# Queue order around the macaron kernel's second attention: feed-forward units spread over eight drain rounds, the layer norm moved one round earlier, the low part of x ahead of the low part of y

## The chip, the cores and the metric

One NeuronCore of one Trainium2 chip runs the whole program. The metric is the device time in microseconds (us) of one execution; the time of a kernel is the median of its runs.

## The reference, cut to what matters

The input x has 8192 tokens of 256 channels. Six residual stages follow each other: a gated feed-forward with 4-bit quantization, a decaying linear attention, the same feed-forward again, a ternary feed-forward, a linear attention with a compressive memory, and the ternary feed-forward again. The change touches the fifth stage and the beginning of the sixth.

```python
def _L1_attn_ref(hidden_states, w_q, w_k, w_v, w_o, gate, memories, memory_norms):
    q, k, v = (proj(w_q), proj(w_k), proj(w_v))
    sq = elu1(q)
    sk = elu1(k)
    out_m = jnp.einsum('bhsd,mhde->mbhse', sq, memories)
    rel = jnp.einsum('bhsd,mhd->mbhs', sq, memory_norms)
    out_m = out_m / jnp.clip(rel, EPS, None)[..., None]
    weights = jax.nn.softmax(rel.mean(axis=-1), axis=0)
    mem_out = jnp.einsum('mbhse,mbh->bhse', out_m, weights)
...
    num = jnp.einsum('bhsd,bhsde->bhse', sq, kv_cum)
    den = jnp.clip(jnp.einsum('bhsd,bhsd->bhs', sq, k_cum), EPS, None)
    local = num / den[..., None]
    out = g * mem_out + (1.0 - g) * local
    return out @ w_o.T

def _L1_ffn_ref(x, W1, b1, W2, b2):
    h = jnp.einsum('bsd,fd->bsf', x, _ternary(W1)) + b1
    h = jax.nn.gelu(h, approximate=False)
    return jnp.einsum('bsf,df->bsd', h, _ternary(W2)) + b2
...
    x = x + _L1_attn_ref(_layernorm(x, axis=-1), ...)
    x = x + 0.5 * _L1_ffn_ref(_layernorm(x, axis=-1), ...)
```

## The kernel before, in words

x stays in SBUF as 64 tiles of 128 tokens; four tiles are a chunk. Each engine runs a list of instructions written out by hand, in order, and semaphores tie the lists together. Most products are made from a high and a low part of an operand, so a tile that PE transposes into PSUM is first copied by ACT as the high part (`XTH`, `YTH`), and then DVE subtracts that from PSUM to get the low part (`XTL`, `YTL`).

The second attention is a software pipeline of rounds n = 0 to 75. With j = n % 4, round n does on PE, in this order: `values(n)` and, 12 tiles behind, `out_proj(n - 12)`; `keys(n)`; `grow`, `numerators`; `recall(n - 10)` (the memory part); `denominators`, `scores(n)`, `enter`; transposes of tile n - 2's numerators and of y of tile n - 11 into one pair of banks called "l"; at j = 0 the transposes of the next chunk of x (`turn_x`); at j = 1 and 2 halves of the next chunk's projection (`attn1_proj`); at n % 8 == 1 (n > 8) a sum over eight tiles ("w") for the softmax weights. From n = 64 on there are no new tiles: round 64 has what is left of tile 63, and rounds 65 to 75 are the drain, which has `recall` (to round 73), `out_proj` and the transposes of y, and, between them, the first units of the next feed-forward.

All of it shares three pairs of PSUM banks, handed out in the order of `slots1()`; in rounds 66 and later only two pairs, in turn, since the feed-forward needs two banks. `attn1_take` makes PE wait until the last user of the pair is emptied. Worked out from that order: from round 12 on, the second half of `recall(n - 10)` takes the pair of `values(n)`, which ACT's copy L2009 (`VK1`) empties. `out_proj(z)` also waits for `s_yl`, which DVE's L2139 (`YTL`) gives in the round before. In rounds 67 to 73 the first half of `recall` needs the pair that `residual` (DVE L2069) of the round before empties, and its second half the pair that L2139 of the round before empties; `out_proj` then needs the first half of the same round's `recall` emptied by DVE (L2086, `recalled`).

A feed-forward unit (`ffn1_unit`, one per 128 of 1024 hidden channels of a chunk) is four matmuls of 512 columns (L1559, L1560) on PE, a gelu (L1599) and a copy (L1603) on ACT, and a subtraction (L1625) on DVE; from unit 5 on PE also does the eight matmuls (L1576, L1578) of the unit five before. Units 0 to 10 of stage 5 are placed in the drain rounds by the table `beside`; unit 11 and all later ones follow the last `out_proj`. Units 5, 6 and 7 are followed on ACT by one row each of a layer norm, and so is unit 8; units 0 to 2 on DVE by its statistics.

`norm` (ACT L267, four activations) writes the normalized next chunk, `XN`, that `turn_x` transposes at the next j = 0. `low(i)` (DVE L290, two subtractions) makes the low part of that chunk once ACT has copied the high part (L286). It is needed by `attn1_proj` a round later.

Of the kernel before, what the change touches and what calls it, by code (L numbers as in the profile page):

```python
# [7 lines left out]
NT = 64  # L8
# [17 lines left out]
def macaron(nc, x, wgu, wd, wqkv, bqkv, bv, wo0, bo0, gam, w1, b1, w2, b2, aw, awo, gate, mem, mnorm, cst, out):  # L26
    pwd = nc.dram_tensor("pw_scratch", [16, 256], F32, kind="Internal").ap()
    top = ExitStack()
    with top:
# [225 lines left out]
        def norm(act, S, i, rows=range(4)):  # L255
            F = 16 * S + i
            b = F % 2
            if 0 in rows:
                act.wait_ge(s_nb, 2 * F + 2)
                if S in (0, 2) and i:  # L260
                    act.wait_ge(s_qxv, 8 * S + i)
                elif S in (1, 3) and i == 0:
                    act.wait_ge(s_qxv, 8 * (S - 1) + NS)
                elif F:
                    act.wait_ge(s_xt, 2 * F)
            for j in rows:
                t = act.activation(XN[:, j, :], X[:, 4 * i + j, :], ACT.Identity,  # L267
                                   scale=rs[b][:, j:j + 1], bias=nb[b][:, j:j + 1])
            if 3 in rows:
                t.then_inc(s_xn, 1)  # L270
# [1414 lines left out]
        after1 = lambda j: 15 * (j // 16) + min(j % 16 + 1, 15)  # L1685

        beside = {66: (0, 1), 67: (2, 3), 68: (4, 5), 69: (6, 7), 70: (8,), 71: (9,), 72: (10,)}
        AHEAD = 11

        def slots1():
# [79 lines left out]
        def attn1_pe(pe):  # L1771
# [124 lines left out]
            for n in range(NT + FAR + 2):  # L1896
                m, p, r, y, z, i, j = n - 1, n - 2, n - FAR, n - FAR - 1, n - FAR - 2, n // 4 + 1, n % 4
                if n > NT and r < NT:
                    recall(r)
                for u in beside.get(n, ())[:1]:  # L1900
                    ffn1_unit(pe, 5, u)
                if n < NT:
                    values(n)
                if z >= 0:
                    out_proj(z)
                if n < NT:
                    keys(n)
                if n == 0:
                    turn_x(i)
                if n == 1:  # L1910
                    pe.wait_ge(s_xd, 64 * 3 + 64)
                if 0 <= m < NT:
                    grow(m, 0)
                    numerators(m)
                if n <= NT and r >= 0:
                    recall(r)
                if 0 <= m < NT:
                    denominators(m)
                    grow(m, 1)
                if n < NT:  # L1920
                    scores(n)
                if 0 <= m < NT:
                    enter(m)
                if 0 <= p < NT or 0 <= y < NT:
                    bank = attn1_take(pe, "l", n)
                if 0 <= p < NT:
                    pe.wait_ge(n_nu, p + 1)
                    for c in range(3):
                        t = pe.transpose(bank[:, 128 * c:128 * c + 128], NU[p % 2][:, 128 * c:128 * c + 128],
                                         ident[:, :])  # L1930
                    t.then_inc(n_lx, 1)
                if 0 <= y < NT:
                    pe.wait_ge(n_p, 3 * y + 3)
                    for k in range(2):
                        t = pe.transpose(bank[:, 512 + 128 * k:640 + 128 * k], Y[y % 2][:, 128 * k:128 * k + 128],
                                         ident[:, :])
                    t.then_inc(n_yx, 1)
                for u in beside.get(n, ())[1:]:
                    ffn1_unit(pe, 5, u)
                if 0 < n <= NT and j == 0:  # L1940
                    turn_x(i)
                if n < NT and i < NS and j in (1, 2):
                    attn1_proj(pe, i, j - 1)
                if n % 8 == 1 and 8 < n < NT + 2:
                    bt = n // 8 - 1
                    bank = attn1_take(pe, "w", bt)
                    pe.wait_ge(n_le, p + 1)
                    for c in range(8):
                        raw = L[:, (8 * bt + c) % 10, 256:336].rearrange("p (q c) -> p q c", q=4)
                        t = pe.matmul(bank[:, 0:64], ones[:, :], raw[:, :, 4:20], start=(c == 0), stop=(c == 7))  # L1950
                    t.then_inc(n_rsum, 1)
# [9 lines left out]
        def attn1_act(act):  # L1961
# [40 lines left out]
            for n in range(NT + FAR + 2):  # L2002
                m, p, y, i, j = n - 1, n - 2, n - FAR - 1, n // 4 + 1, n % 4
                if n < NT:
                    act.wait_ge(n_vk, n + 1)
                    if n > 1:
                        act.wait_ge(n_up, after1(2 * (n - 2) + 1))
                        act.wait_ge(d_v1[n % 2], 64 * ((n - 2) // 2) + 64)
                    act.activation(VK1[n % 2][:, 0:512], pair1("v", n)[:, 0:512], ACT.Copy).then_inc(n_vke, 1)  # L2009
                    if j == 2:  # L2010
                        norm(act, *chunk(64 + i + 1))
                if n == 66:
                    act.wait_ge(n_lx, NT)
                for u in beside.get(n, ())[:1]:
                    ffn1_unit_act(act, 5, u)
                if 0 <= m < NT:
                    act.wait_ge(n_it, m + 1)
                    if m > 1:
                        act.wait_ge(n_lx, m - 1)
                    act.activation(NU[m % 2][:, :], PS[6][:, 0:384], ACT.Copy).then_inc(n_nu, 1)  # L2020
                if 0 <= y < NT:
                    act.wait_ge(n_yx, y + 1)
                    if y:
                        act.wait_ge(n_op, y)
                    act.activation(YTH[:, :], half1(1, "l", n)[:, 0:256], ACT.Copy).then_inc(s_yh, 1)
                for u in beside.get(n, ())[1:]:
                    ffn1_unit_act(act, 5, u)
                if 0 <= p < NT:
                    act.wait_ge(n_lx, p + 1)
                    if p > 9:  # L2030
                        act.wait_ge(n_p, 3 * (p - 10) + 3)
                    act.activation(L[:, p % 10, 0:256], half1(0, "l", n)[:, 0:256], ACT.Copy)
                    act.activation(L[:, p % 10, 256:336].rearrange("p (q c) -> p q c", q=4),
                                   half1(0, "l", n)[:, 256:384].rearrange("p (q c) -> p q c", q=4)[:, :, 0:20],
                                   ACT.Copy).then_inc(n_le, 1)
                if n <= NT and j == 0:
                    turn_x(i)
                if n < NT and i < NS:
                    if j in (1, 2):
                        proj(i, j - 1)  # L2040
                    if j == 3:
                        keys(i)
                if n % 8 == 1 and 8 < n < NT + 2:
                    bt = n // 8 - 1
                    act.wait_ge(n_wz, 7 * bt + 3)
                    act.activation(RM[bt % 2][:, :], RM[bt % 2][:, :], ACT.Exp).then_inc(n_wx, 1)
        def attn1_dve(dve):
            v3 = lambda a: a.rearrange("p (g m b) -> p g m b", m=4, b=2)
            vm = lambda a: a.rearrange("p (g m b) -> p g b m", m=4, b=2)
# [21 lines left out]
            def mask(n, g):  # L2071
                dve.wait_ge(n_sc, 2 * n + g + 1)
                if n:
                    dve.wait_ge(n_av, n)
                tab = bass.AP(tensor=TR[:, :].tensor, offset=TR[:, :].offset,
                              ap=[list(TR[:, :].ap[0]), [0, 2], [0, 4], [1, 64]])
                dve.tensor_tensor(
                    a1A[:, 512 * g:512 * g + 512].rearrange("p (q a t) -> p q a t", q=2, a=4),
                    pair1("s", n, g).rearrange("p (q c) -> p q c", q=2)[:, :, 0:256].rearrange(
                        "p q (a t) -> p q a t", a=4), tab, ALU.mult).then_inc(n_am, 1)  # L2080
# [14 lines left out]
            for n in range(NT + FAR + 2):  # L2095
# [31 lines left out]
                    recalled(r, 1)  # L2127
                if 0 < n <= NT:
                    state(2 * n - 1)
                for u in beside.get(n, ())[:1]:  # L2130
                    ffn1_unit_dve(dve, 5, u)
                if n > NT:
                    residual(z)
                if n < NT:
                    mask(n, 0)
                    mask(n, 1)
                if 0 <= y < NT:
                    dve.wait_ge(s_yh, NT + y + 1)
                    dve.tensor_tensor(YTL[:, :], half1(1, "l", n)[:, 0:256], YTH[:, :].bitcast(F32),  # L2139
                                      ALU.subtract).then_inc(s_yl, 1)  # L2140
                if n <= NT and j == 0:
                    low(i)
                for u in beside.get(n, ())[1:]:
                    ffn1_unit_dve(dve, 5, u)
                if 0 <= p < NT:
                    dve.wait_ge(n_le, p + 1)
# [171 lines left out]
```

## Time and profile before

| | us |
|---|---|
| median of 3 runs (lowest, highest) | 2545.09 (2544.83, 2546.74) |
| the profiled execution, its own time | 2546.74 |
| its span in the trace | 2544.7 |
| PE matmuls busy | 2413.9 |
| DVE busy | 1889.8 |
| ACT busy | 1407.7 |

Rounds can be counted by ACT's 64 copies L2009: the one of round n is the (n+1)th. The first starts at 1654.41 us and the last, of round 63, at 2225.49 us. The first instruction of unit 11 starts at 2300.95 us.

### The profile page before, as it was taken

Reading aid. Unit: us, or ns where it says so; the run is one execution under the profiler, and the core shown is the slowest. Engines: PE = TensorE matmul, PEld = TensorE weight load, DVE = VectorE, ACT = ScalarE, POOL = GpSimd, SP = SyncE. Lnnn points to the kernel's source line nnn. Section 1 sums busy time; section 2 is a strip of 40 time slices with the busy share of each in tenths; the row PEclk is TensorE's granted clock in tenths of the full one; section 3 lists DMA queues with packets and bytes.
Section 4 is the critical chain, followed back from the end, with each engine's and each line's share of the span. In section 5 each row is a group of like instructions: output and inputs, shape, how many; then the busy total and the mean of one; then the engine's idle time right before and its main releaser. Section 6 shows DMA issues by size and latency. Waiting matters only on the chain.

```text
span 2544.7 us, 78166 instructions
## 1 busy us (share of the span) xinstructions
PE 2413.9 (95%) x32232; PEld 2119.3 (83%) x32232; DVE 1889.8 (74%) x4447; ACT 1407.7 (55%) x2427; POOL 1287.2 (51%) x1392
## 2 busy tenths in 40 slices
PE   4999999999999979999999999989999999989999
PEld 3888888888888868888888899877888888868998
DVE  8999899677778789999985766546666666665664
ACT  4555555533434435556655888854444445436886
POOL 5878888621212138889996333113443444444331
PEclk9999999999999999999999999999999999989999
DMA  5000000001111110000000000000000000000111
GB/s 190 1 7 1 1 1 1 1 23 24 24 24 25 24 48 1 1 1 1 1 1 1 19 1 2 1 20 18 17 18 18 17 18 17 18 4 26 34 34 42
DMA packets 67728, 46.12 MB, mean 18 GB/s; under 512 B 13216, under 2 KB 66352, under 8 KB 67376
## 3 DMA queue, kind: packets, MB, share of 16 engines
q1 hardware_dynamic: 67376, 41.13, 5.7%
q8 instruction: 257, 4.21, 0.7%
q14 instruction: 95, 0.78, 0.1%
HBM read 15.91 MB, written 8.40 MB: 10 GB/s over the span
## 4 chain that ended last, share of the span: by engine, by line
PE 85%; DVE 5%; issue 3%; POOL 3%; ACT 3%; DMA 0%; SPq 0%; DVEq 0%; ACTq 0%; POOLq 0%
PE ps L46 14%; PE ps L48 13%; PE ps L47 13%; PE ps L1576 5%; PE ps L1578 5%; PE ps L1559 5%; PE ps L1560 4%; PE ps L628 3%; PE ps L280 3%; PE ps L1856 3%; PE ps L1135 2%; PE ps L1167 2%; PE ps L1816 1%; PE ps L1891 1%; PE ps L1874 1%
## 5 line engine op out<-in xcount | busy, mean ns | idle before, releaser
L1625 DVE TENSOR_TENSOR gHl<-gHf,gHh 128x512 fp32r<-128x512 f32 x256 | 186.3, 728 | 192.9 <-ACT gHh L1603 192.8
L46 PE MATMUL ps<-WGH,XTH 128*128 128x512 f32 (+1 forms) x768 | 300.0, 391 | 7.3 <-ACT fSG L697 4.5
L247 POOL TENSOR_SCALAR ve<-mv 128x4 f32<-128x4 f32 x96 | 22.0, 229 | 558.8 <-DVE mv L237 554.5
L48 PE MATMUL ps<-WGL,XTH 128*128 128x512 f32 (+1 forms) x768 | 290.2, 378 | 0.0
L47 PE MATMUL ps<-WGH,XTL 128*128 128x512 f32 (+1 forms) x768 | 289.4, 377 | 0.0
L697 ACT ACTIVATE fSG<-ps 128x704 f32<-128x704 f32 x128 | 97.0, 758 | 311.2 <-PE ps L48 311.2
L843 POOL TENSOR_TENSOR fHTL<-fHTF,fHTH 128x768 fp32r<-128x768 f32 x128 | 235.8, 1842 | 63.4 <-ACT fHTF L706 63.4
L1576 PE MATMUL ps<-W2T,gHh 128*128 128x256 f32 x1024 | 256.9, 284 | 0.0
L1578 PE MATMUL ps<-W2T,gHl 128*128 128x256 f32 x1024 | 254.3, 282 | 0.0
L1599 ACT ACTIVATE gHf<-ps,B 128x512 f32<-128x512 f32 x256 | 175.9, 687 | 92.2 <-PE ps L1560 88.2
L46 PE MATMUL ps<-WDH,fHTH 128*128 128x256 f32 x768 | 221.8, 289 | 2.6 <-issue 2.6
L48 PE MATMUL ps<-WDL,fHTH 128*128 128x256 f32 x768 | 216.4, 282 | 0.0
L47 PE MATMUL ps<-WDH,fHTL 128*128 128x256 f32 x768 | 216.2, 281 | 0.0
L267 ACT ACTIVATE XN<-X,nb,rs 128x256 f32<-128x256 f32 x384 | 209.4, 590 | 7.7 <-POOL nb L253 7.7
L1559 PE MATMUL ps<-XTH,W1T 128*128 128x512 f32 x512 | 208.6, 407 | 0.4 <-DVE XTL L290 0.4
L1560 PE MATMUL ps<-XTL,W1T 128*128 128x512 f32 x512 | 203.8, 398 | 0.0
L1576 PEld LDWEIGHTS ps<-W2T,gHh 128*128 128x128 f32 x1024 | 194.1, 190 | 10.6
L849 POOL TENSOR_TENSOR fV<-fH,frc 128x704 f32<-128x704 f32 x128 | 178.1, 1391 | 48.8 <-DVE frc L788 48.4
L1578 PEld LDWEIGHTS ps<-W2T,gHl 128*128 128x128 f32 x1024 | 193.4, 189 | 9.2
L855 POOL TENSOR_TENSOR fHX<-fV,fsc 128x704 f32<-128x704 f32 x128 | 178.0, 1390 | 28.3 <-DVE fV L322 28.3
L1603 ACT ACTIVATE gHh<-gHf 128x512 fp32r<-128x512 f32 x256 | 161.7, 632 | 8.2
L46 PEld LDWEIGHTS ps<-WGH,XTH 128*128 128x128 f32 x768 | 145.9, 190 | 23.0 <-ACT fSG L697 6.0
(257 smaller groups left out, 7084.6 us busy)
## 6 DMA issues: line engine op xcount, KB each, us to landing
X<-in_x SPq DMA_DIRECT2D x16, 512.0 KB, 8.8
a0vp<-a0vt SPq DMA_DIRECT2D x256, 32.0 KB
a1vp<-a1vk SPq DMA_DIRECT2D x256, 32.0 KB, 1.9
out<-X SPq DMA_DIRECT2D x16, 512.0 KB, 2.9
tws<-in_w SPq DMA_DIRECT2D x2, 1024.0 KB, 7.8
WN<-in_wgu SPq DMA_DIRECT2D x3, 384.0 KB, 5.6
a0km<-in_wqkv SPq DMA_DIRECT2D x2, 384.0 KB, 3.3
a1pry<-in_aw SPq DMA_DIRECT2D x1, 768.0 KB, 4.6
```

Source lines behind the costliest of these rows:

```text
L46: e.matmul(o, hh, mh, start=first, stop=False)
L47: e.matmul(o, hl, mh, start=False, stop=False)
L48: return e.matmul(o, hh, ml, start=False, stop=last)
L267: t = act.activation(XN[:, j, :], X[:, 4 * i + j, :], ACT.Identity, scale=rs[b][:, j:j + 1], bias=nb[b][:, j:j + 1])
L843: pool.tensor_tensor(HTL[(n - 3) % 2][:, :, :], HTF[:, :, :], HTH[(n - 3) % 2][:, :, :].bitcast(F32), ALU.subtract).then_inc(s_hlo, 1)
L849: pool.tensor_tensor(s3(V[n % 2][:, :]), s3(H[n % 2][:, :]), cast16(rc[n % 2][:, :], 44), ALU.mult).then_inc(s_hv, 1)
L855: pool.tensor_tensor(s3(HX[(n - 1) % 2][:, :]), s3(V[(n - 1) % 2][:, :]), cast16(sc[(n - 1) % 3][:, :], 44), ALU.mult).then_inc(s_hx, 1)
L1559: pe.matmul(up(S, m)[:, :], W1T[:, k, fs], XTH[b][:, k, :], start=(k == 0), stop=False)
L1560: t = pe.matmul(up(S, m)[:, :], W1T[:, k, fs], XTL[b][:, k, :], start=False, stop=(k == 1))
L1576: pe.matmul(o, Hh[S][w][:, js], W2T[:, f, :], start=(f == 0 and j % 2 == 0), stop=False, skip_group_check=True)
L1578: t = pe.matmul(o, Hl[S][w][:, js], W2T[:, f, :], start=False, stop=(f == 7), skip_group_check=True)
L1625: dve.tensor_tensor(Hl[S][m % 8][:, :], Hf[S][m % 4][:, :], Hh[S][m % 8][:, :].bitcast(F32), ALU.subtract).then_inc(s_hl, 1)
```

## The change

The units of `beside` are spread over eight rounds in place of seven, one unit in the even and two in the odd rounds up to 71, and all of a round's units come at the end of the round, behind the transposes and copies of y. Before, the first unit of a round stood between `recall` and `out_proj` on PE, ahead of the copies for y on ACT and ahead of `residual` and `YTL` on DVE. The norm on ACT goes from round j = 2, behind the copy L2009, to the very end of round j = 1. On DVE `low(i)` goes ahead of `YTL` in rounds j = 0. Nothing is computed that was not computed before.

```diff
-        beside = {66: (0, 1), 67: (2, 3), 68: (4, 5), 69: (6, 7), 70: (8,), 71: (9,), 72: (10,)}
+        beside = {66: (0,), 67: (1, 2), 68: (3,), 69: (4, 5), 70: (6,), 71: (7, 8), 72: (9,), 73: (10,)}
@@ attn1_pe
                 if n > NT and r < NT:
                     recall(r)
-                for u in beside.get(n, ())[:1]:
-                    ffn1_unit(pe, 5, u)
                 if n < NT:
                     values(n)
@@ behind the transposes of y
-                for u in beside.get(n, ())[1:]:
+                for u in beside.get(n, ()):
                     ffn1_unit(pe, 5, u)
@@ attn1_act
                     act.activation(VK1[n % 2][:, 0:512], pair1("v", n)[:, 0:512], ACT.Copy).then_inc(n_vke, 1)
-                    if j == 2:
-                        norm(act, *chunk(64 + i + 1))
                 if n == 66:
                     act.wait_ge(n_lx, NT)
-                for u in beside.get(n, ())[:1]:
-                    ffn1_unit_act(act, 5, u)
                 if 0 <= m < NT:
                     act.wait_ge(n_it, m + 1)
@@ behind the copy YTH
-                for u in beside.get(n, ())[1:]:
+                for u in beside.get(n, ()):
                     ffn1_unit_act(act, 5, u)
@@ behind the exponential L2046, the last of the round
+                if n < NT and j == 1:
+                    norm(act, *chunk(64 + i + 1))
@@ attn1_dve
                 if 0 < n <= NT:
                     state(2 * n - 1)
-                for u in beside.get(n, ())[:1]:
-                    ffn1_unit_dve(dve, 5, u)
                 if n > NT:
                     residual(z)
                 if n < NT:
                     mask(n, 0)
                     mask(n, 1)
+                if n <= NT and j == 0:
+                    low(i)
                 if 0 <= y < NT:
                     dve.wait_ge(s_yh, NT + y + 1)
                     dve.tensor_tensor(YTL[:, :], half1(1, "l", n)[:, 0:256], YTH[:, :].bitcast(F32),
                                       ALU.subtract).then_inc(s_yl, 1)
-                if n <= NT and j == 0:
-                    low(i)
-                for u in beside.get(n, ())[1:]:
+                for u in beside.get(n, ()):
                     ffn1_unit_dve(dve, 5, u)
```

## Rows read from the trace of the kernel before

**Rows 1.** The page: busy time, share of the span, instructions.
```profile
PE 2413.9 (95%) x32232; PEld 2119.3 (83%) x32232; DVE 1889.8 (74%) x4447; ACT 1407.7 (55%) x2427; POOL 1287.2 (51%) x1392
```
**Rows 2.** Windows: stretch, its length, busy of PE, PEld, DVE, ACT, POOL; clock; DMA.
```profile
1950.00:2050.00 100.00, 96.99 (x2257) 82.85 (x2257) 65.93 (x163) 47.79 (x105) 40.63 (x61) 1.00 0.07 17
```
**Rows 3.** Waits of PE, 1800 to 2100 us: total, times, longest.
```profile
PE ps L1891 <- ACT a1vk L2009: 5.1, 8, 0.7
```
**Rows 4.** Timeline, rounds 28 and 29: start, duration, engine, line, [idle before, releaser].
```profile
1906.65 0.42 DVE L2139 TENSOR_TENSOR a1ytl<-ps,a1yth 128x256 fp32r<-128x256 f32 x1 [0.86 <-ACT a1yth L2025]
...
1907.54 1.29 DVE L290 TENSOR_TENSOR XTL<-ps,XTH 128x512 fp32r<-128x512 f32 x2 [0.47 <-ACT XTH L286]
1907.60 0.28 PE L46 MATMUL ps<-a1oh,a1yth 128*128 128x256 f32 x1
```
**Rows 5.** Timeline, the change from round 29 to 30.
```profile
1918.56 0.63 ACT L1983 ACTIVATE a1sq<-a1sq 128x512 f32<-128x512 f32 x1
...
1919.55 0.60 ACT L2009 ACTIVATE a1vk<-ps 128x512 f32<-128x512 f32 x1 [0.36 <-PE ps L1801]
...
1920.04 2.06 ACT L267 ACTIVATE XN<-X,nb,rs 128x256 f32<-128x256 f32 x4
...
1920.51 0.73 PE L1891 MATMUL ps<-a1mb,a1sq 32*128 32x128 f32 x16
```
**Rows 6.** Timeline, the change from round 33 (n % 8 == 1) to 34.
```profile
1957.60 0.26 ACT L2046 ACTIVATE a1rm<-a1rm 128x64 f32<-128x64 f32 x1 [2.05 <-DVE a1rm L2172]
1957.77 0.58 ACT L2009 ACTIVATE a1vk<-ps 128x512 f32<-128x512 f32 x1
...
1958.66 0.73 PE L1891 MATMUL ps<-a1mb,a1sq 32*128 32x128 f32 x16
```
**Rows 7.** Timeline, the beginning of round 28.
```profile
1900.94 0.59 ACT L2009 ACTIVATE a1vk<-ps 128x512 f32<-128x512 f32 x1
...
1901.68 0.73 PE L1891 MATMUL ps<-a1mb,a1sq 32*128 32x128 f32 x16 [0.63 <-ACT a1vk L2009]
```
**Rows 8.** Timeline of PE, drain rounds 66 to 75.
```profile
2251.43 0.41 PE L46 MATMUL ps<-a1oh,a1yth 128*128 128x256 f32 x1
...
2256.68 1.24 PE L1891 MATMUL ps<-a1mb,a1sq 32*128 32x128 f32 x16 [2.70 <-DVE a1ytl L2139]
...
2280.82 0.73 PE L1891 MATMUL ps<-a1mb,a1sq 32*128 32x128 f32 x16 [2.25 <-DVE a1ytl L2139]
2281.48 0.50 PE L1559 MATMUL ps<-XTH,W1T 128*128 128x512 f32 x1
...
2282.51 0.28 PE L1576 MATMUL ps<-W2T,gHh 128*128 128x256 f32 x1
...
2286.33 0.94 PE L1891 MATMUL ps<-a1mb,a1sq 32*128 32x128 f32 x16 [1.79 <-DVE a1ytl L2139]
...
2299.53 0.55 PE L46 MATMUL ps<-a1oh,a1yth 128*128 128x256 f32 x1 [1.02 <-DVE a1ytl L2139]
```
**Rows 9.** Timeline of ACT in the drain.
```profile
2251.72 1.28 ACT L1599 ACT_TABLE_LOAD   x1 [2.67 <-PE ps L1560]
...
2282.71 0.69 ACT L1599 ACTIVATE gHf<-ps,B 128x512 f32<-128x512 f32 x1 [3.72 <-PE ps L1560]
2283.43 0.64 ACT L1603 ACTIVATE gHh<-gHf 128x512 fp32r<-128x512 f32 x1
```
**Rows 10.** Timeline of DVE in the drain.
```profile
2284.10 0.77 DVE L1625 TENSOR_TENSOR gHl<-gHf,gHh 128x512 fp32r<-128x512 f32 x1 [1.15 <-ACT gHh L1603]
...
2293.45 1.29 DVE L2086 TENSOR_TENSOR a1P<-ps,a1cf 128x512 f32<-128x512 f32 x2 [0.86 <-DVE a1cf L2117]
```
**Rows 11.** Timeline of PE: single gaps of the other stages, one of six.
```profile
945.14 0.63 PE L280 MATMUL ps<-ident,fXV 128*128 128x128 f32 x4 [1.70 <-DVE XTL L290]
```
**Rows 12.** Windows of PE around such a gap and one in the drain: length, busy, clock, DMA.
```profile
943.00:949.00 6.00, 4.22 (x24) 1.00 0.00 0
2284.00:2290.00 6.00, 4.21 (x30) 0.73 0.01 3
```

## The prediction

> **What bounds the kernel now.** The page comes first: PE matmuls are busy 95% of the span, far ahead of DVE and ACT [rows 1], so what counts is what opens or closes a gap on PE. The windows come next: in the steady part of the second attention, rounds of about 9.5 us, PE is busy 96.99 of 100 us at clock 1.00 [rows 2]. PE's waits there are short; the largest group is `recall` (L1891) behind ACT's copy L2009, 8 times, 0.7 us at most [rows 3]. PE has no slack, and those loops of dependence start and end on PE, so a new wait of PE is hardly given back later. The reader is to look at each of the three moves by one question: whom does PE wait for just there, and how long before PE came had it been ready? The timelines answer that.
>
> **Move 1: `low` ahead of `YTL` (j = 0).** In round 28 DVE does L2139 at 1906.65 for 0.42 us, then the pair L290 from 1907.54 to 1908.83, which must wait for ACT's copies of the high part. PE starts `out_proj` of round 29 at 1907.60 [rows 4]. `out_proj` needs L2139. Once L290 stands ahead of it, L2139 starts at 1908.83 at the earliest and ends at 1909.25. PE starts about 0.15 us behind a release: a copy that ended at 1901.53 let `recall` start at 1901.68 [rows 7]. So `out_proj` starts at 1909.40 and not at 1907.60, 1.80 us later. Who profits? `attn1_proj` needs L290, but it comes a whole round later, and L290 waits for ACT and so starts no earlier than before. There is no gain to set against the loss. Behind the waiting L2139 on DVE stand only the reciprocals of `RC`; behind the waiting PE stands everything. The pattern repeats in rounds 12, 16, ..., 60, which is 13 times: 13 x 1.80 = 23.4 us. In round 64 both `recall` and `out_proj` of round 65 need it; there `recall` comes 2 us later, but DVE's `recalled` only about 0.7 us later, since it had waited for other work. Move 1: **+24 us**. Its bounds: 0 if DVE could do L2139 in the 0.47 us it waits for L286, which its fixed order excludes, up to 26 if a late `residual` costs a little more.
>
> **Move 2: the norm at the end of round j = 1.** Before, its 2.06 us lie behind the copy L2009, in a stretch where ACT waits for PE anyway. After, they lie ahead of that copy, and `recall` (its second half takes the copy's PSUM pair) waits for it. In the even kind of round, ACT's exponential ends at 1919.19 [rows 5]. Neighbouring activations overlap by about 0.1 us (the copy starts at 1919.55, takes 0.60, the norm starts at 1920.04 [rows 5]). So the norm runs 1919.09 to 1921.15, the copy 1921.04 to 1921.64, and `recall` starts at 1921.79 and not at 1920.51: 1.28 us, in rounds 14, 22, ..., 54, six times: 7.7 us. Where n % 8 == 1, the exponential of the weights L2046 ends at 1957.86 and the copy starts right behind it [rows 6]. The norm goes between them: copy to 1960.32, `recall` at 1960.47 and not at 1958.66: 1.81 us, in rounds 18, 26, ..., 58, six times: 10.9 us. Round 62 has no projection ahead of it, so ACT is idle early: 0.3 us. In round 10 it is `scores`, later in the round, that takes the pair: 0.6 us. Rounds 2 and 6: nothing. The copy also starts the DMAs of `VP1`, needed a round later; they shift together with PE. A gain, ACT being free in round j = 2, is worth nothing: it waits for PE there. Move 2: **+19.5 us**, bounds 11 (the six largest alone) and 26 (13 times 2.0). That a copy behind other ACT work stalls `recall` is seen already: in rounds j = 0 it does, for 0.63 us [rows 7].
>
> **Move 3: the units in the drain.** Before, DVE's `YTL` stands behind the first unit's L1625, and so the next `recall` waits for gelu, copy and subtraction: 2.70, 2.25 and 1.79 us [rows 8], 6.7 us together. After, these three waits go. What is late next? The round's last L1625 now stands ahead of the next round's L2086 on DVE, and `out_proj` needs L2086. The length of a round, `out_proj` to `out_proj`, is a chain: `out_proj` and the transposes 0.9; the unit's four matmuls 1.03 (2281.48 to 2282.51 [rows 8]); 0.2 to ACT; gelu and copy 1.36 (2282.71 to 2284.07 [rows 9]); L1625 0.7; the coefficients 0.25; the first half of L2086 0.65 [rows 10]; 0.2 for two handovers: 5.3 us. A second unit adds another 0.94 us of matmuls, and more if the first has its down part in between (another 0.94): 6.7 (units 4, 5) and 7.2 (7, 8). The first two intervals, at half clock, with the table load of 1.28 us [rows 9] and the softmax weights ahead, I put at 8.6 and 8.3. Then 5.3, 6.7, 5.3, 7.2, 5.3, and 5.2 for the last two, which have no `recall`: 51.9 us. Before it was 2299.53 - 2251.43 = 48.1 [rows 8]. The last `out_proj` then runs at the full clock, 0.7 us quicker. Move 3: **+3 us**, from -7 (the three waits go and nothing takes their place) to +8 (half clock throughout the drain). The Trainium skill ("ScalarE: Activation LUTs", What ACT_TABLE_LOAD costs) puts a switch of tables at 2.66 us, with a drain; the trace shows the gelu directly behind a load of 1.28 us, so the row stands. By the page the sum would be 1.4 us higher.
>
> **The clock.** Moves 1 and 2 make 25 new gaps of about 1.3 to 1.8 us. In the trace seven single gaps of 1.4 to 1.8 us bear on it. Six, in other stages, left the clock at 1.00 (one is 1.70 us [rows 11], its window [rows 12]); the one of 1.79 us in the drain [rows 8] was followed by half clock, 0.73 over 6 us, which costs 6 x 0.27 = 1.6 us [rows 12]. One in seven of 25 at 1.6 us is **+6 us**; bounds 0 and 25 x 1.6 = 40.
>
> **The sum:** 24 + 19.5 + 3 + 6 = 52.5 us on the profiled execution's 2546.7 us gives 2599; that execution lies 1.7 above the median of 2545.1, which gives 2597.6. I take **2598 us**.
>
> **The rivals.**
> *Half clock in the attention.* The new gaps lie among matmuls on 32 rows or columns, not among full ones as those six did. If each of them, or most, is followed by half clock, the term of 6 becomes 25 to 40: 2617 to 2632 us. Against it: the 0.63 us waits among the same small matmuls leave it at 1.00.
> *Only one move tells.* Should a later wait absorb one of the two (say `recall`'s stall is taken up by scores and masks), 22 us are left: 2567. Against it: `scores` starts right behind PE's own work in these rounds, and the short waits [rows 3] are too small to absorb anything.
> *No effect.* DVE and ACT find both a place without PE waiting, and the drain comes out even: 2545. It would need the order on each engine not to bind.
> *Faster, by the drain.* The mechanism is that `YTL` no longer waits for the gelu: PE's three waits, 6.7 us, go, and L2086 comes in time; the stalls of moves 1 and 2 don't occur. 2538 us. It decides from the point where the chain of a one-unit round is below PE's own work in it, about 3.5 us (recall 0.7, the chain's 0.9 and 1.03, the down part 0.94); I count 5.3, so even the drain alone is not faster, and it would have to outweigh 43 us besides.
>
> **How the numbers follow.** The forecast, all four terms as worked out within their nearer bounds (2580 to 2616 us): 0.70. Half clock: 0.14. One move alone: 0.08. No effect: 0.04. Faster: 0.04. For 8 in 10 the range goes from 2567, the one-move case, to 2636, the half-clock case with the drain's upper bound. Changes below 0.2% (5 us) can't be told from none. Faster 0.04, the same 0.04, slower 0.92.
>
> **What the profile after would show.** Move 1: at the start of each round j = 1, `out_proj` (L46 from a1yth) with an idle time of 1.8 us, released by DVE a1ytl, 13 times. Move 2: L1891 idle for 1.3 and 1.8 us in turn behind ACT a1vk in rounds j = 2, and ACT's norm ahead of that copy. Move 3: `recall`'s waits for a1ytl gone in the drain, and `out_proj` waiting for DVE a1P or a1pry, 1 to 3 us, in nearly every round; unit 11 starting some 46 us later than before, 3 of it from the drain. The windows of the steady part: PE busy near 92 of 100 us. Wrong would be: no wait on a1ytl in rounds j = 1 (then L2139 is not what `out_proj` waits for), the clock below 0.95 in the steady windows, or a drain below 48 us.

## The result and the profile after

The changed kernel takes 2609.91 us (median of 4 runs, 2605.24 to 2614.76) and the kernel before 2545.91 us on the same chip: ratio 1.0249, 95% interval 1.0225 to 1.0273, so 64 us slower. The forecast was 2598 us, slower, with a range from 2567 to 2636. The profiled execution took 2608.26 us, its span 2606.3. Line numbers have moved a little: after, L2007 is the copy L2009, L2136 is `YTL` (L2139 before), and L2083 is `recalled` (L2086 before).

The windows of the steady part come first, one row of each kernel (stretch, length, busy of PE, PEld, DVE, ACT, POOL, then the clock). Of before:

```profile
1755.00:2215.00 460.00, 443.83 (x10674) 379.92 (x10663) 302.64 (x746) 216.83 (x470) 192.89 (x295) 1.00 0.07 17
```

Of after:

```profile
1755.00:2215.00 460.00, 413.60 (x9608) 352.36 (x9604) 273.17 (x669) 195.83 (x425) 174.66 (x268) 0.97 0.06 16
```

In the same 460 us PE is busy for 30 us less, and its mean clock is 0.97 and no longer 1.00. The waits of PE over the second attention and the drain, 1650 to 2370 us, of after (total, times, longest) say behind whom:

```profile
PE ps L46 <- DVE a1ytl L2136: 27.0, 30, 1.5
PE ps L1891 <- ACT a1vk L2007: 26.1, 26, 1.7
PE ps L46 <- DVE a1P L2083: 9.1, 4, 3.1
PE ps L46 <- DVE a1pry L2083: 8.3, 4, 3.0
...
PE ps L1891 <- DVE a1ytl L2136: 2.2, 1, 2.2
```

and of before, 1650 to 2310 us:

```profile
PE ps L1891 <- ACT a1vk L2009: 8.3, 13, 0.7
PE ps L46 <- DVE a1ytl L2139: 7.9, 18, 1.0
PE ps L1891 <- DVE a1ytl L2139: 7.9, 5, 2.7
```

Each of the three moves has its row. `out_proj` behind `YTL` has grown from 7.9 to 27.0 us (move 1), `recall` behind the copy from 8.3 to 26.1 us (move 2), and the waits of `recall` for `YTL`, 7.9 us, are down to one of 2.2 us, in round 65, while 17.4 us of `out_proj` behind `recalled` have come (move 3).

Round 29 after, which answers to [rows 4] (timelines of DVE and PE):

```profile
1928.40 1.29 DVE L290 TENSOR_TENSOR XTL<-ps,XTH 128x512 fp32r<-128x512 f32 x2 [1.76 <-ACT XTH L286]
1929.61 0.41 DVE L2136 TENSOR_TENSOR a1ytl<-ps,a1yth 128x256 fp32r<-128x256 f32 x1
...
1930.17 0.35 PE L46 MATMUL ps<-a1oh,a1yth 128*128 128x256 f32 x1 [1.54 <-DVE a1ytl L2136]
```

L2136 now starts where L290 ends, and PE 0.15 us behind its end. The idle column says 1.54 us, but the distance of this round's copy from the same one before grows by 1.77 us. Before, the matmul ahead of `out_proj` started at 1907.49 and lasted 0.28 us, while `out_proj` started at 1907.60: 0.17 us of the two were counted together, and that overlap goes too. The round from 29 to 30, which answers to [rows 5]:

```profile
1940.63 0.63 ACT L1981 ACTIVATE a1sq<-a1sq 128x512 f32<-128x512 f32 x1
1941.17 2.06 ACT L267 ACTIVATE XN<-X,nb,rs 128x256 f32<-128x256 f32 x4
1943.14 0.57 ACT L2007 ACTIVATE a1vk<-ps 128x512 f32<-128x512 f32 x1
...
1943.86 0.73 PE L1891 MATMUL ps<-a1mb,a1sq 32*128 32x128 f32 x16 [1.20 <-ACT a1vk L2007]
```

and from 33 to 34, which answers to [rows 6]:

```profile
1983.31 2.06 ACT L267 ACTIVATE XN<-X,nb,rs 128x256 f32<-128x256 f32 x4
1985.28 0.57 ACT L2007 ACTIVATE a1vk<-ps 128x512 f32<-128x512 f32 x1
...
1986.00 0.73 PE L1891 MATMUL ps<-a1mb,a1sq 32*128 32x128 f32 x16 [1.73 <-ACT a1vk L2007]
```

The norm stands between the exponential and the copy, and `recall` is idle for 1.20 or 1.73 us. In the drain, PE of after ([rows 8] before):

```profile
2316.54 0.58 PE L46 MATMUL ps<-a1oh,a1yth 128*128 128x256 f32 x1 [3.06 <-DVE a1P L2083]
...
2324.59 0.39 PE L46 MATMUL ps<-a1oh,a1yth 128*128 128x256 f32 x1 [2.96 <-DVE a1pry L2083]
...
2363.12 0.36 PE L46 MATMUL ps<-a1oh,a1yth 128*128 128x256 f32 x1 [1.02 <-DVE a1ytl L2136]
```

Where the time is, all kernels side by side. The stretches run between starts: of the copy of rounds 0, 12 and 63, of the first `out_proj` of rounds 66 and 75, and of unit 11. All values are of the one profiled execution of each kernel, in us.

| kernel | round 0 at | rounds 0 to 12 | 12 to 63 | 63 to 66 | drain 66 to 75 | to unit 11 | unit 11 to end |
|---|---|---|---|---|---|---|---|
| before | 1654.4 | 96.0 | 475.1 | 25.9 | 48.1 | 1.4 | 243.8 |
| after | 1654.6 | 100.8 | 529.4 | 24.3 | 54.1 | 0.8 | 242.4 |
| e1_low | 1650.6 | 97.4 | 500.5 | 23.9 | 47.7 | 0.8 | 242.4 |
| e2_norm | 1656.7 | 100.2 | 507.7 | 24.9 | 48.0 | 0.8 | 242.4 |
| e4_low_norm | 1655.4 | 99.0 | 528.7 | 26.1 | 46.8 | 1.4 | 243.5 |
| e3_drain | 1649.7 | 96.7 | 473.7 | 25.4 | 56.9 | 1.0 | 243.7 |
| e5_norm_behind | 1655.9 | 96.5 | 472.8 | 25.6 | 46.5 | 1.4 | 243.3 |
| e6_order | 1654.8 | 98.5 | 473.0 | 24.9 | 54.2 | 1.4 | 244.4 |
| e7_table | 1652.0 | 95.4 | 472.6 | 26.1 | 45.5 | 1.4 | 243.1 |
| e8_dve | 1651.1 | 96.6 | 472.0 | 24.6 | 43.3 | 1.4 | 243.4 |
| f1_low_clamp | 1655.3 | 95.7 | 501.7 | 23.8 | 46.0 | 1.4 | 243.1 |
| f2_keys | 1649.5 | 95.1 | 463.6 | 25.1 | 46.5 | 1.4 | 243.1 |
| f3_keys_dve | 1653.7 | 94.8 | 463.7 | 26.1 | 42.5 | 1.4 | 243.2 |
| f4_keys_dve_table | 1655.1 | 97.8 | 466.1 | 25.5 | 45.0 | 1.4 | 243.3 |

Two traces of the same code differ, too. In the six kernels that add no wait to the steady part (before, e3_drain, e5 to e8) rounds 12 to 63 took 472.0 to 475.1 us, and in the seven with the drain of before it took 46.0 to 48.1 us. The trace of before has the largest value both times, so a stall or a loss worked out against it can be up to 3 us too small in the steady part, and a gain in the drain up to 2 us too large.

From before to after: 0.2 + 4.8 + 54.3 - 1.6 + 6.0 - 0.6 - 1.4 = 61.7 us, the difference of the spans. Nearly nine tenths of it is the steady part, where moves 1 and 2 act.

### The profile page after: what moved, and what is told of

The parts are those of the page before. It is cut to its first block, busy times and chain, and to the rows that moved or that the text cites. A ratio compares the mean times of both kernels' runs of the same rounds, so it can differ in the third digit from the quotient of the medians.

```text
span 2606.3 us, 78165 instructions
## 1 busy us (share of the span) xinstructions
PE 2432.0 (93%) x32232; PEld 2133.7 (82%) x32232; DVE 1891.5 (73%) x4447; ACT 1406.7 (54%) x2427; POOL 1285.8 (49%) x1392
## 4 chain that ended last, share of the span: by engine, by line
PE 83%; DVE 6%; ACT 5%; issue 4%; POOL 2%; DMA 0%; SPq 0%; DVEq 0%; ACTq 0%; POOLq 0%
PE ps L46 13%; PE ps L48 13%; PE ps L47 13%; PE ps L1576 5%; PE ps L1578 5%; PE ps L1559 5%; PE ps L1560 4%; PE ps L628 3%; PE ps L280 3%; PE ps L1856 3%; PE ps L1135 2%; PE ps L1167 2%; PE ps L1891 2%; PE ps L1874 1%; PE ps L1154 1%
## 5 line engine op out<-in xcount | busy, mean ns | idle before, releaser
L1625 DVE TENSOR_TENSOR gHl<-gHf,gHh 128x512 fp32r<-128x512 f32 x256 | 184.9, 723 | 195.8 <-ACT gHh L1603 195.7
L843 POOL TENSOR_TENSOR fHTL<-fHTF,fHTH 128x768 fp32r<-128x768 f32 x128 | 235.8, 1842 | 61.7 <-ACT fHTF L706 61.7
L2014 ACT ACTIVATE a1nu<-ps 128x384 f32<-128x384 f32 x64 | 31.4, 491 | 271.0 <-PE ps L1880 271.0
```

Source lines behind the costliest of these rows:

```text
L843: pool.tensor_tensor(HTL[(n - 3) % 2][:, :, :], HTF[:, :, :], HTH[(n - 3) % 2][:, :, :].bitcast(F32), ALU.subtract).then_inc(s_hlo, 1)
L1625: dve.tensor_tensor(Hl[S][m % 8][:, :], Hf[S][m % 4][:, :], Hh[S][m % 8][:, :].bitcast(F32), ALU.subtract).then_inc(s_hl, 1)
```

## The experiments

Times are medians; the ratio is to the kernel before, run beside it on the same chip, with its 95% interval. The median of before was 2543.2 us beside e1 to e8 and 2542.1 us beside f1 to f4.

**e1_low, move 1 alone.**

```diff
+                if n <= NT and j == 0:
+                    low(i)
                 if 0 <= y < NT:
                     dve.wait_ge(s_yh, NT + y + 1)
...
-                if n <= NT and j == 0:
-                    low(i)
```

> Only move 1 of the change (DVE's low, L290, ahead of YTL). Theory (order on DVE delays out_proj): out_proj of each round j = 1 stands idle about 1.5 us behind YTL, 13 times, each round 1.8 us late, 24 us in all, plus 0 to 6 us where the clock falls: 2568 to 2576 us. Rival (the stall is absorbed later in the round): within 3 us of the kernel before.

Measured 2572.94 us, 1.0118 (1.0090 to 1.0146). Rounds 12 to 63 take 25.4 us more than before. Its waits of PE, 1750 to 2250 us:

```profile
PE ps L46 <- DVE a1ytl L2141: 24.5, 27, 1.5
PE ps L1891 <- ACT a1vk L2009: 7.7, 12, 0.7
```

The first row holds the 13 long waits, the second is that of before. 13 x 1.77 = 23.0 us is the stall, 2.4 us is left for the clock. The trace is of the fastest execution, 2565.29 us at a mean clock of 0.989; the other three took 2570 to 2579 us at 0.985 or 0.986, so in them the clock probably cost more. The stall is not absorbed; the rival falls.

**e2_norm, move 2 alone.**

```diff
-                    if j == 2:
-                        norm(act, *chunk(64 + i + 1))
...
                     act.activation(RM[bt % 2][:, :], RM[bt % 2][:, :], ACT.Exp).then_inc(n_wx, 1)
+                if n < NT and j == 1:
+                    norm(act, *chunk(64 + i + 1))
```

> Only move 2 (the norm at the very end of ACT's round j = 1, so ahead of the copy VK1 of round j = 2). Theory: recall of rounds j = 2 idle behind that copy, 1.2 us in six rounds and 1.7 us in six, 19.5 us in all, plus 0 to 6 us of clock: 2564 to 2572 us. Rival (ACT has slack enough, its share of busy time being 55%): within 3 us of the kernel before.

Measured 2582.38 us, 1.016 (1.014 to 1.018), more than either theory gave. Its waits of PE, 1750 to 2265 us:

```profile
PE ps L1891 <- ACT a1vk L2009: 25.9, 25, 1.7
PE ps L46 <- DVE a1ytl L2140: 4.9, 15, 0.3
```

The waits are as expected. Rounds 12 to 63 take 32.6 us more. The twelve stalls at the forecast's size, 6 x 1.28 + 6 x 1.81, and 0.3 in round 62 are 18.8 of them; about 14 us are left. The windows of PE around round 18 show where they are:

```profile
1808.00:1818.00 10.00, 9.94 (x182) 1.00 0.05 13
1818.00:1828.00 10.00, 8.33 (x154) 0.66 0.06 16
1828.00:1838.00 10.00, 9.67 (x226) 1.00 0.06 16
```

and its timeline what half clock does to small matmuls, 1.99 us for the 32 of `scores` in place of 1.12 us:

```profile
1819.67 1.04 PE L1891 MATMUL ps<-a1mb,a1sq 32*128 32x128 f32 x16 [1.73 <-ACT a1vk L2009]
...
1822.06 1.99 PE L1856 MATMUL ps<-a1sq,a1km 32*128 32x64 f32 x32
```

Between rounds 12 and 63 the clock fell five times, to half for 6.8 us each, which is 34 us; 14 us lost in 34 us of half clock is 0.4 us for each.

**e3_drain, move 3 alone:** the new `beside`, and on all three engines

```diff
-                for u in beside.get(n, ())[:1]:
-                    ffn1_unit(pe, 5, u)
...
-                for u in beside.get(n, ())[1:]:
+                for u in beside.get(n, ()):
                     ffn1_unit(pe, 5, u)
```

> Only move 3 (units spread over eight rounds and placed at the end of the round). Theory: out_proj of the drain waits for DVE's L2086, which stands behind the unit's L1625; first out_proj of round 66 to the last one takes 52 to 54 us in place of 48, so 2549 to 2552 us. Rival: the waits of recall for YTL go and nothing takes their place, 6.7 us faster, 2539 us.

Measured 2553.36 us, 1.0042 (1.0026 to 1.0059). The drain takes 56.9 us. Waits of PE, 2225 to 2305 us:

```profile
PE ps L46 <- DVE a1P L2082: 8.4, 4, 2.5
PE ps L46 <- DVE a1pry L2082: 7.8, 4, 2.6
```

Eight rounds, eight waits of `out_proj` for `recalled`. The mechanism is the one expected, the size is larger, 56.9 us where 52 to 54 were expected.

**e4_low_norm, moves 1 and 2 together,** the first two diffs.

> Moves 1 and 2 without move 3. Theory (the stalls add up, since both sit on PE at different places of the round; the clock falls more often with both): 24 + 19.5 = 43.5 us and 5 to 15 us of clock, 2594 to 2604 us. Rival (one hides in the other): 2570 us. If the clock falls only where both stalls are there, e1 and e2 show 1.00 in the steady windows and this one 0.93 to 0.97.

Measured 2602.93 us, 1.0235 (1.0217 to 1.0254). In rounds 12 to 63 the two stalls add up: 23.0 + 18.8 = 41.8 of 53.6 us. What is left for the clock is 11.8 us, no more than in e2_norm alone, and both traces have 34.1 us of half clock in these rounds, so the clock's part does not add. That the clock falls only where both stalls are there is wrong: e2_norm shows 0.96 in the window from 1755 to 2215 us, e1_low 0.99, this one 0.97.

**e5_norm_behind.** The norm in the earlier round, but behind the copy.

```diff
-                    if j == 2:
+                    if j == 1:
                         norm(act, *chunk(64 + i + 1))
```

> The norm goes to round j = 1 as in move 2, but right behind the copy VK1 of that round and not at the round's end. Theory (it is the place ahead of a copy that costs, not the round): recall has no new wait, time within 3 us of the kernel before. Rival (an earlier norm itself collides, with the y copies or with POOL's spread): 10 to 20 us slower.

Measured 2541.95 us, 0.9993 (0.9978 to 1.0007). The waits of `recall`, 1750 to 2230 us, are those of before:

```profile
PE ps L1891 <- ACT a1vk L2009: 8.3, 13, 0.7
```

The earlier round costs nothing; what costs is the place ahead of the copy.

**e6_order,** the diff of e3_drain with the table of before.

> Half of move 3: the old table of units, but all units at the end of the round on the three engines. Theory (the order is what costs in the drain: L1625 ahead of L2086): about 52 us from the first to the last out_proj of the drain in place of 48, 3 to 5 us slower than before. Rival (the table costs, not the order): within 1 us of before.

Measured 2551.67 us, 1.0034 (1.0020 to 1.0048), 8.5 us slower where 3 to 5 were expected; the drain takes 54.2 us. **e7_table,** the new table with the order of before:

> The other half of move 3: the new table, the old order (first unit between recall and out_proj). Theory: rounds with one unit take about 6 us and rounds with two 5.7 us in the old order, and the new table has more one-unit rounds: about 50.5 us, 2 us slower. Rival (the table is the whole cost): 4 us or more slower.

Measured 2538.47 us, 0.9983 (0.9970 to 0.9996); the drain takes 45.5 us, just below the 46.0 to 48.1 of the kernels with the table of before. So the order is the cost of move 3. My account of the table was wrong: I had expected 2 us slower, and it came out no slower, if anything faster.

**e8_dve.** The order of before on PE and ACT; on DVE alone the units stand behind `residual` and `YTL`.

```diff
-                for u in beside.get(n, ())[:1]:
-                    ffn1_unit_dve(dve, 5, u)
                 if n > NT:
                     residual(z)
...
-                for u in beside.get(n, ())[1:]:
+                for u in beside.get(n, ()):
                     ffn1_unit_dve(dve, 5, u)
```

> The old table and the old order on PE and ACT; on DVE alone residual and YTL go ahead of the round's first L1625 and its layer norm statistics. Theory: recall then waits only for YTH and YTL; its waits of 2.70, 2.25 and 1.79 us shrink by 0.7 to 1.5 us each, 3 to 4.5 us faster than before (2541 to 2543 us). Rival (L1625 and the statistics then delay L2086 by as much): no change.

Measured 2538.14 us, 0.9981 (0.9969 to 0.9994), 5 us faster where 3 to 4.5 were expected; the drain takes 43.3 us. PE in two of its rounds with one unit:

```profile
2270.33 0.73 PE L1891 MATMUL ps<-a1mb,a1sq 32*128 32x128 f32 x16 [1.02 <-DVE a1ytl L2137]
...
2275.14 0.73 PE L1891 MATMUL ps<-a1mb,a1sq 32*128 32x128 f32 x16 [1.02 <-DVE a1ytl L2137]
```

`recall`'s waits of 2.25 and 1.79 us [rows 8] are 1.02 now, and the round is 4.8 us long. The same DVE order is part of e6_order, which is slower: there PE and ACT too do the unit at the end of the round, here they still do the first one between `recall` and `out_proj`. DVE's L1625 in a round of e8_dve,

```profile
2274.57 0.42 DVE L2137 TENSOR_TENSOR a1ytl<-ps,a1yth 128x256 fp32r<-128x256 f32 x1 [0.21 <-ACT a1yth L2025]
2274.91 1.25 DVE L1625 TENSOR_TENSOR gHl<-gHf,gHh 128x512 fp32r<-128x512 f32 x1
```

and of e6_order:

```profile
2277.91 0.69 DVE L1625 TENSOR_TENSOR gHl<-gHf,gHh 128x512 fp32r<-128x512 f32 x1 [1.47 <-ACT gHh L1603]
```

In the first L1625 finds its operand ready. In the second it waits 1.47 us, and the next round's `recalled` waits behind it. The new order on DVE has a price too. From 2225 to 2310 us `recall`'s waits for `YTL` go from 7.9 us before to 3.8, but those of `out_proj` for `recalled` go from 2.1 to 4.7 us.

**f1_low_clamp.** e1_low with one more DVE instruction ahead of `YTL` in rounds j = 0.

```diff
                 if n <= NT and j == 0:
                     low(i)
+                if 0 <= p < NT and j == 0:
+                    clamp(p)
                 if 0 <= y < NT:
```

> Move 1 and, in rounds j = 0, DVE's tensor_scalar on RC (L2150, 0.2 us) ahead of YTL as well, so that out_proj's gap of 1.5 us becomes about 1.75 us, as long as recall's largest gap in e2_norm. Theory (the clock falls where the gap lies among the small matmuls around recall, not by its length): at most 2 of the 13 gaps are followed by half clock, rounds 12 to 63 take about 3 us more than in e1_low. Rival (the length of the gap alone decides): about as often as in e2_norm, 5 falls or more, and 10 us or more on top of e1_low.

Measured 2568.31 us, 1.0111 (1.0089 to 1.0133); rounds 12 to 63 take 501.7 us, 1.2 more than in e1_low. The gap grew to 1.66 us only and not to the 1.75 that was aimed at. A gap of `out_proj`, and the windows of PE around it and around the one gap that a fall followed:

```profile
1918.69 0.36 PE L46 MATMUL ps<-a1oh,a1yth 128*128 128x256 f32 x1 [1.66 <-DVE a1ytl L2152]
```

```profile
1912.00:1922.00 10.00, 8.34 (x231) 1.00 0.08 19
1796.00:1806.00 10.00, 8.34 (x197) 0.83 0.06 16
```

Counted by the granted clock in rounds 12 to 63 of the traces: behind the gaps of 1.73 us before `recall` the clock fell in 4 of 6 cases in e2_norm, 4 of 6 in e4_low_norm and 4 of 6 in the changed kernel, 12 of 18. Behind those of 1.20 us, 3 of 18. Behind the gaps of 1.54 us before `out_proj`, 3 of 39 (e1_low, e4_low_norm, the changed kernel), and of 1.66 us here, 1 of 13. Three falls more follow no such gap: one in e4_low_norm, one here, and one in f4_keys_dve_table below, which has none of the new gaps. Each kernel has one trace; the mean clock of e1_low's other executions was lower than in its trace, so its 1 of 13 may be too few.

At one place, `recall`, the longer gaps are followed by half clock more often. Between the two places, gaps that differ by 0.07 us are followed by it in 2 of 3 cases among the 32-row and 32-column matmuls around `recall`, and in 1 of 13 between the full-size matmuls around `out_proj`. That points to the place, as the theory had it, and the 10 us of the rival did not come. Two things are not shown: that the last 0.07 us do not matter, and that it is the size of the matmuls, and not something else in those rounds, that makes the difference.

**f2_keys.** The lesson of move 2 turned round.

```diff
                     act.activation(VK1[n % 2][:, 0:512], pair1("v", n)[:, 0:512], ACT.Copy).then_inc(n_vke, 1)
+                    if j == 0 and n:
+                        keys(i - 1, (1,))
...
                     if j == 3:
-                        keys(i)
+                        keys(i, (0,))
```

> The lesson of move 2 turned round: of the four activations of keys (L1991) at the end of ACT's round j = 3 the last two go behind the copy VK1 of the next round. Theory (what stands ahead of that copy is what recall waits for): its 13 waits of 0.63 us vanish, 8 us faster than before. Rival (the masked keys are then late for scores, or another wait takes the place): no change or slower.

Measured 2528.80 us, 0.9952 (0.9940 to 0.9964), 13 us faster where 8 were expected. ACT and PE in a round j = 0, which answers to [rows 7]:

```profile
1891.36 0.60 ACT L2010 ACTIVATE a1vk<-ps 128x512 f32<-128x512 f32 x1 [0.18 <-PE ps L1801]
1891.86 1.32 ACT L1991 ACTIVATE a1km<-a1sk,par 128x512 f32<-128x512 f32 x2
...
1892.31 0.73 PE L1891 MATMUL ps<-a1mb,a1sq 32*128 32x128 f32 x16
```

`recall` starts without a wait, and rounds 12 to 63 take 463.6 us; the kernels with the steady part of before lie between 472.0 and 475.1. In 11 of the 13 rounds `recall` follows the one before it 0.70 to 0.73 us sooner than in the trace of before, which makes 9 us; where the rest of the 13 us comes from was not tried.

**f3_keys_dve,** f2_keys with e8_dve:

> f2_keys together with e8_dve (residual and YTL ahead of the first L1625 in the drain). If they touch different waits, their gains add: 8 and 5 us, 12 to 13 us faster than before.

Measured 2527.41 us, 0.9938 (0.9927 to 0.9950), 15 us faster than before and with the lowest median of all; the drain takes 42.5 us. The medians of f2 and f3 are only 1.4 us apart and their intervals overlap, so that the gains add is seen in the trace's stretches (3.9 us in the drain), not in the times. **f4_keys_dve_table,** with the new table as well:

> f3_keys_dve with the new table of units. If the table's small gain in e7_table is its own, 2 to 4 us faster than f3_keys_dve; if it came only from a unit less between recall and out_proj in round 66, or from the clock, no difference.

Measured 2529.65 us, 0.9953 (0.9940 to 0.9966), not faster; the drain takes 45.0 us. The table has no gain of its own here. Whether e7_table's 0.17% is one stays open.

## Why the prediction was right, point by point

**Move 1: right in place and size.** 1.80 us for each of 13 rounds were forecast, 1.77 us measured, 23.0 us against 23.4; e1_low has it alone.

**Move 2: right in place and size as a stall.** 1.28 and 1.81 us were forecast. The idle times are 1.20 and 1.73 us; the distance of `recall` from the same one before grows by 1.28 us in round 22 and by 1.79 us in rounds 18 and 58. e5_norm_behind shows that it is the place ahead of the copy.

**Move 3: the mechanism was right, the size too small.** The waits for `YTL` went and `recalled` took their place. The chain gave 51.9 us for the drain; it takes 54.1 in the changed kernel, 54.2 in e6_order and 56.9 in e3_drain. What is off is the length of the rounds. For one unit 5.3 us were put, and the rounds took 5.5, 5.2 and 5.8. For two units with a down part it was 7.7 in place of 7.2, the first intervals were 7.5 and 8.1 where 8.6 and 8.3 were put, and the last two rounds took 6.6 and not 5.2. The largest miss is the round with units 4 and 5, 7.8 us (2330.06 to 2337.90) where 6.7 were put. The working's own terms, 5.3 and 0.94, give only 6.2 there. And the clock was half for 3.4 us from 2329.8, so that `out_proj` alone, up to the transposes, took 1.45 us in place of 0.81 a round later.

Alone, move 3 costs 0.42%, 10 us, which is more than its upper bound of 8. On top of the other two it costs 64.0 - 59.8 = 4 us, by the medians of the changed kernel and of e4_low_norm less those of before beside them. The intervals of these two differences reach about 6 and 5 us to either side, so 4 us can't be told from 10 or from none.

**The clock: the term that was mis-sized.** 6 us were forecast, by one gap in seven of 25 at 1.6 us each. In rounds 12 to 63 the changed kernel has 54.3 - 41.8 = 12.5 us of it, by the trace of before, and up to 3 us more by the other traces of the same steady part. The number of falls was off more than their price: 7 of the 25 gaps were followed by half clock and not 3 or 4 (four of 1.73 us, one of 1.20 and two of 1.54), 3.4 to 10.2 us long and 37.5 us together, at 1.8 us each.

The ratio came from seven gaps. The six that left the clock at 1.00 lay among full-size matmuls; the seventh, ahead of `recall` in the drain, was followed by half clock. One more gap among small matmuls stood in the trace of before and was left out: 1.42 us in round 0, ahead of the small matmuls of `scores` (L1856, at 1655.12). In 7 of the 14 traces here the clock falls 1 to 2 us after this gap has ended; in the other seven, before among them, it falls 3.4 to 4.4 us after, near a second gap of 2.56 us. The rival of half clock in the attention had named the place, with every gap or most at 25 to 40 us in all. It holds in place, for 4 of the six gaps of 1.73 us, and not in size.

Rounds 0 to 12 took another 4.8 us, of which the forecast had 0.6. There the clock was half from 1657.4 us for 13.7 us, and before from 1658.7 for 3.4. That the change did this is not shown. f4_keys_dve_table, which has neither move 1 nor move 2, has the same 13.7 us, and e4_low_norm, which has both, has 3.4.

**The sum.** 52.5 us were forecast; 62 are seen in the spans and 64 in the medians, inside the range. The stalls came out as forecast, 41.8 us in rounds 12 to 63 where 42.3 were put. What is missing is the clock there (12.5 and not 6), rounds 0 to 12 (4.8 and not 0.6) and the drain (6.0 and not 3, less 3.6 us by which three stretches without a forecast of their own were shorter). So unit 11 starts 63 us later than before and not 46, and PE is busy 90 of 100 us in the steady windows and not 92. The rivals of one move alone, of no effect and of a faster drain are excluded: e1_low, e2_norm and e4_low_norm show that both stalls stay and add.

## What to carry to other kernels

Ask of each instruction moved on an engine with idle time not how long it is but what stands behind it and who waits for that: a norm of 2 us, 13 times, costs nothing behind the copy and 19 us of stalls ahead of it, and half a `keys` moved behind the same copy gained 13 us. The subtraction nobody needs for a round belongs behind the one that PE needs next. Where a wait is taken away on one engine by a new order, keep the cover that its neighbours had, that is, work that PE can do while DVE catches up: the new order helped on DVE alone and harmed on all three engines.

## What the runs showed of the hardware that was not expected

A single gap of 1.73 us on PE was followed by half clock in 12 of 18 cases among matmuls of 32 rows or columns, one of 1.20 us there in 3 of 18, and one of 1.66 us before full-size matmuls in 1 of 13. Half clock cost 0.3 to 0.4 us per us here (12.5 us in 37.5 in the changed kernel, 14 in 34 in e2_norm). Two stalls a round apart brought no more half clock than the worse of them alone (34.1 us in rounds 12 to 63 both in e4_low_norm and in e2_norm). And the second attention, ahead of which all kernels are the same, began between 1649.5 and 1656.7 us in the profiled executions, 7 us of spread that no edit here made.
